# Layer 3 decoder of a four-layer graph network: split float32r passes on quarter-head pieces

## The reference, cut to what matters

```python
Xh = X.reshape(n, H, D).transpose(1, 0, 2)          # H = 4 heads, D = 128
Xw = einsum('hnd,hde->hne', Xh, W)
sig = sigmoid(f1[:, :, None] + f2[:, None, :])
att = masked_softmax(adj * sig, adj != 0)
Xa = einsum('hij,hjd->hid', att, Xw)                # encoder
Xn = batchnorm(Xa as n x 512)
emb = batchnorm(elu(Xn @ enc_mlp_W.T + b) + Xn)
Y = einsum('hij,hjd->hid', att, emb by heads)       # decoder
Y = elu(einsum('hnd,hed->hne', Y, W))
out = batchnorm(elu(Y @ dec_mlp_W.T + b) + Y)
```

## Time and profile before

| what | us |
|---|---|
| median of 3 runs | 3646.69 (3634.74 to 3658.13) |
| the profiled execution | 3645.72 |
| its span in the trace | 3643.9 |
| TensorE busy | 3184.7 (87%) |
| VectorE busy | 2335.3 (64%) |
| ScalarE busy | 1718.8 (47%) |
| mean granted TensorE clock | 0.954 |

### The profile page before, as it was taken

The page is one execution under the profiler, slowest core; times in us unless marked ns, Lnnn a source line. Parts: engine busy times, 40 slices in busy tenths (PEclk is TensorE's granted clock), DMA queues, the critical chain, the costliest instruction groups (busy, mean ns, idle before and its releaser), DMA issues. The chain is left out here.

```text
span 3643.9 us, 36993 instructions
## 1 busy us (share of the span) xinstructions
PE 3184.7 (87%) x13715; PEld 2198.1 (60%) x13715; DVE 2335.3 (64%) x3070; ACT 1718.8 (47%) x1553; POOL 261.6 (7%) x441
## 2 busy tenths in 40 slices
PE   5799999999978799994888885999999966999994
PEld 4533333333323677773677774888888825888883
DVE  5598989888866466664666663888888643122226
ACT  0288888888852111112344434888888512000002
POOL 0000000000002011110000001001000000000003
PEclk9999999999999899997999997999999988999997
DMA  7500000000012566767222225667676522866654
GB/s 281 201 16 9 16 8 15 15 8 15 7 46 96 207 232 241 280 232 283 94 99 104 99 93 202 263 247 278 246 276 247 231 90 113 337 267 272 271 211 127
DMA packets 119274, 580.73 MB, mean 159 GB/s; under 512 B 13376, under 2 KB 21795, under 8 KB 95312
## 3 DMA queue, kind: packets, MB, share of 16 engines
q1 hardware_dynamic: 96528, 443.44, 32.2%
q0 software_dynamic: 22592, 135.19, 10.3%
HBM read 374.87 MB, written 203.71 MB: 159 GB/s over the span
## 5 line engine op out<-in xcount | busy, mean ns | idle before, releaser
L517 PE MATMUL bank<-dist,hf 128*65 128x512 f32 (+2 forms) x2112 | 830.8, 547 | 64.2 <-ACT dist L479 64.2
L517 PEld LDWEIGHTS bank<-dist,hf 128*65 128x65 f32 x2112 | 277.3, 138 | 609.7 <-issue 457.0
L1379 PE MATMUL bank<-pt,HA 128*128 128x256 f32 x1936 | 505.2, 381 | 3.3 <-DMA HA<-features 3.3
L479 ACT ACTIVATE dist<-dist 128x1408 f32<-128x1408 f32 (+1 forms) x352 | 453.3, 1322 | 1.4
L1568 PE MATMUL bank<-w,EM 128*128 128x256 f32 x1936 | 425.9, 380 | 12.6 <-DMA w<-weights 12.6
L1568 PEld LDWEIGHTS bank<-w,EM 128*128 128x128 f32 x1936 | 368.9, 191 | 63.2 <-DMA w<-weights 12.8
L410 DVE TENSOR_TENSOR dist<-msk,sB 128x1408 f32<-128x1408 uint8 (+1 forms) x208 | 325.3, 1564 | 74.8 <-PE bank L517 65.9
L470 ACT ACTIVATE dist<-dist,neg_t 128x1408 f32<-128x1408 f32 (+1 forms) x208 | 295.8, 1422 | 146.3 <-DVE dist L410 146.3
L1379 PEld LDWEIGHTS bank<-pt,HA 128*128 128x128 f32 x1936 | 328.7, 191 | 27.0 <-DMA HA<-features 3.6
L1367 PE MATMUL bank<-idt,v 128*128 128x128 f32 x1936 | 301.5, 276 | 43.1 <-ACT v L1253 33.3
L1306 DVE COPY pt<-bank 128x512 f32<-128x512 f32 (+1 forms) x440 | 264.6, 630 | 113.0 <-PE bank L1367 111.0
(11 more groups left out here) (162 smaller groups left out, 4445.1 us busy)
## 6 DMA issues: line engine op xcount, KB each, us to landing
w<-weights SPq DMA_DIRECT2D x44, 2816.0 KB, 9.8
weights<-pt SPq DMA_DIRECT2D x220, 512.0 KB, 3.8
al<-in_adj_cols SPq DMA_DIRECT2D x22, 1408.0 KB, 8.2
at<-in_adj_tiles SPq DMA_DIRECT2D x22, 1408.0 KB, 7.9
rows<-in_adj_rows SPq DMA_DIRECT2D x22, 1408.0 KB, 6.4
HB<-in_adj_rows POOLq DMA_DIRECT2D x22, 1354.0 KB, 7.7
rows_low<-HB POOLq DMA_DIRECT2D x22, 1354.0 KB, 5.9
rows<-rows_low POOLq DMA_DIRECT2D x22, 1354.0 KB, 7.5
```

What stands on the lines that cost most here:

```text
L479: act.activation(d[:, 0:VALID[c]], d[:, 0:VALID[c]], ACT.Exp, scale=-1.0).then_inc(p_ready, 1)
L517: mm = pe.matmul(sums_bank(hh, k)[0:FW, 0:hi - a * P], hf[hh][:, m, :], d[:, a * P:hi], start=(m == 0), stop=(m == T - 1))
L1379: t = pe.matmul(acc_t[n % 2][:, 0:P2], HA[:, m, h * D3:(h + 1) * D3], pt[n % 2][:, m, :, :].rearrange("p r n -> p (r n)"), start=(m == 0), ...
```

## The change

The embeddings are kept as two float32r tensors: `EH`, the copy of every tile by ScalarE, and `EL`, VectorE's difference of the PSUM value and `EH`. In the decoder each head's weights are loaded in four pieces of 6, 6, 5 and 5 tiles into a ring of five (`WS`). ScalarE copies each piece to float32r (`split`, into a ring of four, `HS`), VectorE subtracts the copy from the piece in place (`rest`), and TensorE runs three float32r matmuls of 256 columns for each tile in place of one float32 matmul. The inverse sums come for each head on its own, behind its pieces. `dw` is loaded behind the first head's pieces, and TensorE waits for it after the first piece. `mul` follows the first piece of a head. Counts of four semaphores go on from the block before (`M1`), and the orders of ScalarE and VectorE are laid out anew: three pieces are split ahead. The diff, cut to its core:

```diff
@@ -1404,7 +1404,7 @@
-        EM = sb(tail, "EM", [P, T, D])
+        EH, EL = sb(tail, "EH", [P, T, D], F32R), sb(tail, "EL", [P, T, D], F32R)
...
@@ -1450,9 +1450,8 @@
                         for t in range(4 * c, min(4 * c + 4, T)):
-                            if t % 2:
-                                act.wait_ge(em_mm, t + 1)
-                                act.activation(EM[:, t, :], bank[t % 8][:, :], ACT.Copy).then_inc(em_act, 1)
+                            act.wait_ge(em_mm, t + 1)
+                            act.activation(EH[:, t, :], bank[t % 8][:, :], ACT.Copy).then_inc(em_act, 1)
...
@@ -1491,9 +1490,9 @@
                         for t in range(4 * c, min(4 * c + 4, T)):
-                            if t % 2 == 0:
-                                dve.wait_ge(em_mm, t + 1)
-                                dve.tensor_copy(EM[:, t, :], bank[t % 8][:, :]).then_inc(em_dve, 1)
+                            dve.wait_ge(em_act, t + 1)
+                            dve.tensor_tensor(EL[:, t, :], bank[t % 8][:, :], EH[:, t, :].bitcast(FP32), ALU.subtract)\
+                                .then_inc(em_dve, 1)
...
                         if t >= 8:
-                            pe.wait_ge(em_act if t % 2 else em_dve, (t - 8) // 2 + 1)
+                            pe.wait_ge(em_dve, t - 7)
...
-            RING = 4
-            w = [sb(ph, f"w{k}", [P, T, P2]) for k in range(RING)]
-            w_in = [sem(f"w_in{k}") for k in range(RING)]
+            PIECES = [(0, 6), (6, 12), (12, 17), (17, T)]
+            NPC = len(PIECES)
+            WS, HS = 5, 4
+            w = [sb(ph, f"w{k}", [P, 6, P2], F32R) for k in range(WS)]
+            whi = [sb(ph, f"whi{k}", [P, 6, P2], F32R) for k in range(HS)]
+            w_in = [sem(f"w_in{k}") for k in range(WS)]
             dw = sb(ph, "dw", [128, KT, D])
-            riB = [sb(ph, f"riB{k}", [P, H3, P2]) for k in (0, 1)]
+            riB = [sb(ph, f"riB{k}", [P, P2]) for k in (0, 1)]
...
-            att_done, at_ready, e1_ready, u1_ready, y_ready = (sem(f"dec_{k}") for k in ("att", "at", "e1", "u1", "y"))
-            z_done, e_ready, s_ready, h_ready = (sem(f"mlp2_{k}") for k in ("z", "e", "s", "h"))
+            whi_ready, wlo_ready, piece_done = (sem(f"dec_{k}") for k in ("hi", "lo", "piece"))
+            at_ready, e1_ready, u1_ready, y_ready = (sem(f"dec_{k}") for k in ("at", "e1", "u1", "y"))
+            M1 = KT * NCH
...
                 def _(sp):
                     for n in range(HEADS):
                         p, h = divmod(n, H3)
-                        if h == 0:
-                            if p >= 2:
-                                sp.wait_ge(at_ready, H3 * (p - 1))
-                            sp.dma_start(riB[p % 2][:, :, :].rearrange("p h n -> p (h n)"),
-                                         ri_dram[p].rearrange("u n -> (u n)").partition_broadcast(P))\
-                              .then_inc(ri_in[p % 2], 16)
-                        if n >= RING:
-                            sp.wait_ge(att_done, n - RING + 1)
-                        sp.dma_start(w[n % RING][:, :, :], weights[n]).then_inc(w_in[n % RING], 16)
+                        for x, (a, b) in enumerate(PIECES):
+                            k = NPC * n + x
+                            if k >= WS:
+                                sp.wait_ge(piece_done, k - WS + 1)
+                            sp.dma_start(w[k % WS][:, 0:b - a, :].bitcast(FP32), weights[n][:, a:b, :]).then_inc(w_in[k % WS], 16)
+                        if n >= 2:
+                            sp.wait_ge(at_ready, n - 1)
+                        sp.dma_start(riB[n % 2][:, :], ri_dram[p, 2 * h:2 * h + 2, :].rearrange("u n -> (u n)")
+                                     .partition_broadcast(P)).then_inc(ri_in[n % 2], 16)
                         if n == 0:
                             sp.dma_start(dw[:, :, :], dec_w).then_inc(dw_in, 16)
...
                 def _(pe):
-                    def attend(n):
-                        h, k = n % H3, n % RING
-                        pe.wait_ge(w_in[k], 16 * (n // RING + 1))
-                        if n >= 2:
+                    def attend(n, x):
+                        h, k = n % H3, NPC * n + x
+                        a, b = PIECES[x]
+                        if x == 0 and n >= 2:
                             pe.wait_ge(at_ready, n - 1)
-                        for m in range(T):
-                            t = pe.matmul(acc_t[n % 2][:, 0:P2], EM[:, m, h * D3:(h + 1) * D3], w[k][:, m, :],
-                                          start=(m == 0), stop=(m == T - 1))
-                        t.then_inc(att_done, 1)
+                        pe.wait_ge(wlo_ready, k + 1)
+                        into = acc_t[n % 2][:, 0:P2]
+                        for m in range(a, b):
+                            hi, lo = whi[k % HS][:, m - a, :], w[k % WS][:, m - a, :]
+                            pe.matmul(into, EH[:, m, h * D3:(h + 1) * D3], hi, start=(m == 0), stop=False)
+                            pe.matmul(into, EH[:, m, h * D3:(h + 1) * D3], lo, start=False, stop=False)
+                            t = pe.matmul(into, EL[:, m, h * D3:(h + 1) * D3], hi, start=False, stop=(m == T - 1))
+                        t.then_inc(piece_done, 1)
...
                     for n in range(HEADS):
-                        attend(n)
-                        if n == 0:
-                            pe.wait_ge(dw_in, 16)
-                        if n >= H3 + 1:
-                            mul((n - 1) // H3 - 1, (n - 1) % H3)
+                        for x in range(NPC):
+                            attend(n, x)
+                            if n == 0 and x == 0:
+                                pe.wait_ge(dw_in, 16)
+                            if x == 0 and n >= H3 + 1:
+                                mul((n - 1) // H3 - 1, (n - 1) % H3)
                     mul(PAIRS - 2, KT - 1)
...
                 @block.scalar
                 def _(act):
+                    def split(k):
+                        a, b = PIECES[k % NPC]
+                        act.wait_ge(w_in[k % WS], 16 * (k // WS + 1))
+                        if k >= HS:
+                            act.wait_ge(piece_done, k - HS + 1)
+                        act.activation(whi[k % HS][:, 0:b - a, :], w[k % WS][:, 0:b - a, :].bitcast(FP32), ACT.Copy)\
+                           .then_inc(whi_ready, 1)
+
...
-                        act.wait_ge(z_done, n + 1)
+                        act.wait_ge(z_done, M1 + n + 1)
                         if n >= 2:
-                            act.wait_ge(s_ready, n - 1)
+                            act.wait_ge(s_ready, M1 + n - 1)
...
+                    for k in range(HS - 1):
+                        split(k)
                     for n in range(HEADS):
-                        first(n)
+                        split(NPC * n + 3)
+                        if n > 0:
+                            first(n - 1)
+                        if n + 1 < HEADS:
+                            split(NPC * n + 4)
                         if n >= H3 + 1:
                             second((n - 1) // H3 - 1, (n - 1) % H3)
+                        if n + 1 < HEADS:
+                            split(NPC * n + 5)
+                            split(NPC * n + 6)
+                    first(HEADS - 1)
...
                 def _(dve):
+                    def rest(k):
+                        a, b = PIECES[k % NPC]
+                        dve.wait_ge(whi_ready, k + 1)
+                        dve.tensor_tensor(w[k % WS][:, 0:b - a, :], w[k % WS][:, 0:b - a, :].bitcast(FP32),
+                                          whi[k % HS][:, 0:b - a, :].bitcast(FP32), ALU.subtract).then_inc(wlo_ready, 1)
+
                     def first(n):
-                        p, h = divmod(n, H3)
-                        dve.wait_ge(att_done, n + 1)
-                        dve.wait_ge(ri_in[p % 2], 16 * (p // 2 + 1))
+                        dve.wait_ge(piece_done, NPC * (n + 1))
+                        dve.wait_ge(ri_in[n % 2], 16 * (n // 2 + 1))
                         if n >= 2:
                             dve.wait_ge(y_ready, n - 1)
-                        dve.tensor_tensor(at[n % 2][:, :], acc_t[n % 2][:, 0:P2], riB[p % 2][:, h, :], ALU.mult)\
+                        dve.tensor_tensor(at[n % 2][:, :], acc_t[n % 2][:, 0:P2], riB[n % 2][:, :], ALU.mult)\
                            .then_inc(at_ready, 1)
 
...
+                    for k in range(HS - 1):
+                        rest(k)
                     for n in range(HEADS):
-                        first(n)
+                        if n > 0:
+                            first(n - 1)
+                        rest(NPC * n + 3)
+                        if n > 0:
+                            first_end(n - 1)
+                        if n + 1 < HEADS:
+                            rest(NPC * n + 4)
                         if n >= H3 + 1:
```

(28 more changed lines are left out.)

## The result

| | us |
|---|---|
| before, median of 5 | 3646.69 (3634.74 to 3658.13) |
| after, median of 5 | 3617.62 (3617.15 to 3629.66) |
| ratio after / before | 0.9927, 95% interval 0.9898 to 0.9956 |
| forecast | 3587 (3566 to 3636) |

The change is faster by 0.7%, and the interval leaves out 1. That is about half of what was forecast, and less than the 1% that the prediction asked of a difference. The profiled execution took 3617.15 us, its span 3615.4.

A forecast was written before the change was run, and what follows sets the result against it. TensorE was taken to bound the decoder. Head 0 ending at 3095, 33 us for heads 1 to 4 and 381.4 for the rest end it at 3509.4, 59.4 us less: 3587 us, range 3566 to 3636.

The forecast's parts named there:

- The ring: Decoder's weight pieces: a loop of 10.4 us against 12.2 us for five pieces, 1.8 us left, costed at nothing.
- the ring is too short: Rival, decoder loads: landing over about 6 us costs 4/5 us a head per further microsecond; about 3625 us, chance 0.10.
- The pass: Decoder matmuls: a single float32r pass of 256 columns takes 0.122 us, 66 of them a head.
- the unhidden load: Rival, decoder passes: weight load not overlapped or pass not single, 0.216 us each; 3858 us, chance 0.05.
- shared reading: Rival, decoder passes: weight load and stream share one reading rate, 0.139 us a pass; 3636 us, chance 0.09.
- TensorE at 9.78 us a head: Decoder head: 66 passes of 0.122 us plus 1.73 us of `mul`, 9.36 to 10.9 over the ends.
- VectorE: Decoder: needs 9.35 us a head, hidden by 0.4 us; as the rival that sets the head, 3571 us, chance 0.13.
- ScalarE: Decoder: copies of 5.5 us and two exponentials, 6.4 us a head in all, hidden.
- Embeddings: Embeddings' stage: 0.3 us more at each of five joints and 0.7 for the last subtraction, +2.2 us.
- The start: Decoder's start: TensorE waits for `dw` until 3087.2, cold clock costs about 2 us, head 0 ends at 3095; no gain.
- Heads 1 to 4: Decoder heads without `mul`: 8.05 us of passes, taken as 8.3 us each with a refilling ring, 33 us in all.
- heads 5 to 43: Decoder's steady stretch: 39 heads of 9.78 us, 381.4 us in all.

The follow-up runs named there:

- e5: The changed kernel with `mul`'s four products put one behind each piece and the second layer's finish moved to the next head: 3595.94 us, ratio 0.9846.
- e3: The changed kernel with each load after the first five bringing only one of its piece's tiles: 3581.17 us in one run.
- e7: The changed kernel with six piece buffers and two passes, the product of the embeddings' low part left out: 3557.56 us in one run.
- e6: The changed kernel with only the finish of the second layer's block moved to the next head, TensorE's order kept: 3625.5 us in one run.

## Why the prediction was wrong

What failed is one step, "The ring": "It fits, barely, so I cost it at nothing in steady state." Of its loop of 10.4 us, the landing of 5.0 us was the mis-sized term. It was scaled down from whole-head loads, which were issued one at a time, 11 us apart. The pieces are issued in bursts, 1.8 us apart, and each needs 2.0 to 2.4 us of all DMA engines (an estimate, worked out at e5), so the third waits for two others: 6.8 us for the larger pieces and up to 7.3 for the third, where 5.0 was taken. The prediction had the engines' share (0.7) and the ends of the pieces (18 or 15 passes, and `mul` behind the first), but took the mean as proof that nothing queues.

The third load is a head's first piece, and for this piece the loop can be laid out. In means over heads 6 to 42 of the change, from the last matmul of piece k - 5: to the issue 0.3 us, landing 7.3, copy 1.5, subtraction 1.8, three short waits 0.3, passes 2.1, in all 13.3. TensorE at its own pace takes 11.8 for the same stretch (e3), not the 12.2 that the prediction had as a mean of all pieces. The 1.5 us between them hold the gap before the first piece twice, so 0.7 us a head, which is what was measured. With a landing of 5.0 the same parts add up to 10.9, and there would be no gap. The queues on ScalarE and VectorE, which the prediction feared would take nearly all of its 1.8 us, cost this piece 0.05; the second and third piece do wait 1.0 and 0.7 us for VectorE, but TensorE is busy then.

The rival "the ring is too short" named the mechanism, gave it 0.10 and priced it at about 3625; 3617.6 was measured. That chance was too small for a step called "barely".

Point by point:
- The pass: 0.122 taken, 0.120 measured, single passes. Right. The weight loads lie beside the matmuls (183.75 us of them beside 190.56 of matmuls from 3300 to 3500), so neither the 0.216 of the unhidden load nor the 0.139 of shared reading showed. The rule of the Trainium skill ("TensorE: Matmul & The Clock Gate", "The mechanism"; the prediction named the section behind it) that a load overlaps only with matmuls of another row group doesn't hold here.
- TensorE at 9.78 us a head: right as a bound, 9.66 with the ring of six. It was the second latest, behind the ring.
- VectorE: 1.751 and 1.487 us for the subtractions, as worked out (1.755, 1.489). But the durations, 8.9 us in a head by the sum, fill only 150.59 / 160 x 9.03 = 8.5 us in e7: in 114 of 178 pairs of neighbours there the second starts some 0.08 us before the first ends, where gaps of 0.04 were added. The floor is at most 9.0, not 9.35. It stayed hidden.
- ScalarE: 1.487 and 1.274 us, as worked out; hidden.
- Embeddings: +2.1 us, forecast +2.2. The last subtraction ends a block that now begins its loads at 3076.28:

```profile
3075.32 0.69 DVE L1494 TENSOR_TENSOR EL<-bank,EH 128x512 fp32r<-128x512 f32 x1 [0.20 <-ACT EH L1454]
3076.28 0.81 SPq L1555 DMA_DIRECT2D w<-weights  x2
```

- The start: the wait for `dw` behind the first piece was there:

```profile
3083.91 0.58 PE L1574 MATMUL bank<-whi,EH 128*128 128x256 f32 x1 [9.27 <-DVE w L1648]
...
3089.93 0.58 PE L1574 MATMUL bank<-whi,EH 128*128 128x256 f32 x1 [1.80 <-DMA dw<-in_dec_w]
```

  It ended at 3089.9, not 3087.2, of which 2.5 us is the later start of the stage. The clock stayed at half until 3096.0 (the mean is 0.63 from 3085 to 3100). At half clock a pass takes 0.213 us, three of them 0.64:

```profile
3090.74 0.41 PE L1574 MATMUL bank<-whi,EH 128*128 128x256 f32 x1
...
3091.38 0.42 PE L1574 MATMUL bank<-whi,EH 128*128 128x256 f32 x1
```

  So the first 28 of the 48 passes behind the wait lost 0.093 each, 2.6 us, where 2 was taken; what piece 0 lost was hidden by the wait. From the first load to head 1 it is 22.1 us, forecast 21.1, before 22.9.
- Heads 1 to 4: 8.3 forecast, 10.04 measured, by the ring. With six buffers they are 8.49, with one-tile loads 7.92.

With the ring of six the forecast of 3587 is met by 3585.6 (a ratio of 0.982, forecast 0.984). The other terms were right to within 5 us each, and their errors partly cancel: heads 5 to 43 take 4.7 us less than the forecast's 381.4, and the part behind them 3.1 less than before; the start takes 1.3 more, heads 1 to 4 0.9. That kernel is the version to keep.

## What to carry to other kernels

- A ring of pieces has to be costed by its worst piece: lay out the moments at which buffers come free, and add up what stands on the DMA engines at that moment; and take the time that the consumer needs between the same two pieces, not an average. A mean share of 0.7 says nothing on a burst of three loads.
- Where a budget fits "barely", the chance of the rival belongs near one half, and one more buffer is the first thing to try: here 6 KB per partition, 2 of them freed by finishing one step in place, were worth more than the whole change (a ratio of 0.982 in place of 0.993).
- When a unit of work is cut in four, also spread what stands between the units: one product behind each piece won 0.9 us a head with no memory at all.

## What was not expected of the hardware

- Less work for TensorE made the heads longer: with two passes in place of three and a ring of five, heads went from 10.39 to 10.83 us. Stretches at half clock, where a pass takes 0.213 us against 0.120, gave back 1.2 of the 2.6 us saved, and longer waits for the loads 1.9.
- A float32r pass of 256 columns takes 0.120 us, 0.012 more than half of the float32 instruction's 0.216, and more than the 0.115 at most of the projection's instructions; why it is neither 0.116 nor 0.125 stays open.
- The larger loads landed in 5.3, 6.8 and 6.6 us with rings of four, five and six, and in 8.3 us in the two-pass kernel with six. It isn't the depth of the ring alone: with five buffers and the same bytes, issuing them at even distances took the larger from 7.0 (e6) to 6.0 us (e5).
- The same rate costs more of the DMA engines in pieces: 295 GB/s at a share of 0.89, where whole heads came at 296 GB/s with 0.74; why is open.
